# Layer 1 of a graph-attention kernel: the last five rows of the sorted tiles placed behind the last masks, with the closing of the last dense group between them

## The reference

```
# adj: 8192 x 8192, about 8 neighbours in each row, and the node itself
h = relu(layernorm(x));  Wh = h @ W
x = x + leaky_relu(softmax(where(adj, e_left + e_right.T, -1e9)) @ Wh, 0.2)       # layer 0
h = relu(layernorm(x))
e = leaky_relu(h @ a[:d] + (h @ a[d:]).T, 0.01)
x = x + softmax(where(adj, e, -9e15)) @ h                                         # layer 1
```

## Time and profile before

| | before |
|---|---|
| median of 3 runs (lowest, highest) | 1690.48 us (1688.31, 1691.74) |
| the profiled execution | 1689.47 us |
| its span, first to last instruction | 1687.3 us |
| busy: PE, DVE, ACT, POOL | 1551.5, 1255.9, 989.5, 562.5 us |
| first gather of layer 1 starts, last one starts | 1070.41, 1668.87 us |

### The profile page before, as it was taken

How to read it: one execution, slowest core, us unless ns; L and a number is a source line. 1 busy time by engine, 2 the same in 40 slices (tenths; PEclk the granted TensorE clock), 3 DMA queues, 4 the chain that set the end, 5 groups by cost and what they waited for, 6 DMA issues and landing times. The chain is left out here.

```text
span 1687.3 us, 37172 instructions
## 1 busy us (share of the span) xinstructions
PE 1551.5 (92%) x13443; PEld 1321.8 (78%) x13443; DVE 1255.9 (74%) x4759; ACT 989.5 (59%) x1514; POOL 562.5 (33%) x588
## 2 busy tenths in 40 slices
PE   6877999999999999999999999486898999989897
PEld 5645888888888888888888888365687877878786
DVE  6577998998898899887874453696866666666765
ACT  5978656665765566566666661675645445444542
POOL 0000000000000000000014554587777777777776
PEclk9998999999999999999999999798899999999999
DMA  9418989888988898898889994555444444444443
GB/s 318 172 43 341 348 303 364 320 301 313 369 310 300 329 358 310 301 374 319 331 337 385 393 361 112 178 132 153 119 135 114 130 123 129 115 142 117 128 113 107
DMA packets 141700, 406.91 MB, mean 241 GB/s; under 512 B 25857, under 2 KB 91586, under 8 KB 108834
## 3 DMA queue, kind: packets, MB, share of 16 engines
q1 hardware_dynamic: 116114, 335.11, 54.0%
q0 software_dynamic: 25488, 70.77, 14.7%
HBM read 365.39 MB, written 40.41 MB: 241 GB/s over the span
## 5 line engine op out<-in xcount | busy, mean ns | idle before, releaser
L1016 PE MATMUL banks<-HV,adjT 128*128 128x257 f16 x8192 | 938.8, 274 | 18.0 <-DVE adjT L673 10.2
L1016 PEld LDWEIGHTS banks<-HV,adjT 128*128 128x128 fp8e4 x8192 | 791.2, 97 | 150.8 <-DVE HV L703 23.8
L1746 PE MATMUL banks<-Vp,adjp 128*128 128x257 f16 x2304 | 451.9, 278 | 77.5 <-DVE adjp L1561 62.5
L458 ACT ACTIVATE adj_f<-adj_i 128x2048 fp8e4<-128x2048 int32 x256 | 480.1, 1898 | 5.6 <-DMA adj_i<-in_adj 5.5
L1334 POOL DMA_INDIRECT gat<-h_of_layer,rec x393 | 420.5, 1070 | 121.9 <-issue 115.3
L1746 PE MATMUL banks<-Vn,adjn 128*128 128x257 f16 x2304 | 451.0, 278 | 0.0
L1746 PEld LDWEIGHTS banks<-Vp,adjp 128*128 128x128 fp8e4 x2304 | 225.0, 99 | 121.7 <-issue 56.2
L440 POOL DMA_DIRECT2D xr<-x_after_layer x46 | 25.6, 557 | 834.4 <-DVE rank L941 772.5
L1746 PEld LDWEIGHTS banks<-Vn,adjn 128*128 128x128 fp8e4 x2304 | 227.1, 99 | 36.6
L1369 ACT ACTIVATE adjn<-h1bc,nh 128x384 fp8e5<-128x384 f32 x384 | 202.4, 604 | 0.0
L1390 ACT ACTIVATE e<-gat,hb 128x4 f32<-128x4 f32 (+3 forms) x168 | 41.2, 293 | 240.7 <-DMA gat<-h_of_layer,rec 240.5
(11 more groups left out here) (172 smaller groups left out, 1472.6 us busy)
## 6 DMA issues: line engine op xcount, KB each, us to landing
adj_i<-in_adj SPq DMA_DIRECT2D x256, 1024.0 KB, 7.2
h_of_layer<-hh SPq DMA_DIRECT2D x64, 129.0 KB, 6.6
hs<-h_of_layer SPq DMA_DIRECT2D x64, 129.0 KB
xt<-in_x SPq DMA_DIRECT2D x64, 128.0 KB, 7.0
packed_adj<-pk SPq DMA_DIRECT2D x64, 128.0 KB, 6.2
x_after_layer<-x SPq DMA_DIRECT2D x64, 128.0 KB, 7.0
HV<-in_x SPq DMA_DIRECT2D x14, 512.0 KB, 8.8
gat<-h_of_layer,rec POOLq DMA_INDIRECT x393
```

The source lines that it names most:

```text
L458: nc.scalar.activation(adj_f[:, b, q * QC:(q + 1) * QC], adj_i[:, q, :], ACT.Copy, scale=2.0, saturate=False).then_inc(conv_done, 1)
L1016: last = nc.tensor.matmul(acc[b][:, 0:DV], adjT_h[:, b, i, q, :, h], V0[:, jb, s, 0:DV], start=(jb == 0 and s == 0), stop=(jb == T - 1 and ...
L1746: mm = nc.tensor.matmul(bank[2 * i + part][:, 0:DV], m[:, i * P:(i + 1) * P], V[:, j, s, 0:DV], start=(j == 0 and s == 0), stop=(j == T - ...
```

## The change

The table `rows_by` is made with a longer total: `REST` = 1.25 chunk units are added to its divisor. `rows_by[96]` is then 388 in place of 393, and every earlier entry is the old one or up to five rows lower (the first that differs is `rows_by[13]`, 57 for 58). Five rows stand behind the 96 chunks: two of them, then `take_sums` of the last group, one row, `add_negatives`, and the last two with the finishing of the last tiles. ACT's list gets the two calls of `weigh` that go with it.

```
--- before.py
+++ after.py
@@ -1074,6 +1074,7 @@
         LEAD = 3
         FIRST = 1.25
         HEAD = 0.25
+        REST = 1.25
         OUT_LAG = 5
         NOUT = 6
         NACC = 3
@@ -1090,8 +1091,10 @@
         last = [max(k for k in range(len(batch)) if batch[k][0] == m) for m in range(NS)]
         fills = [sum(batch[i][2] - batch[i][1] for i in range(k % NBUF, k + 1, NBUF)) for k in range(len(batch))]
         pace = [max(0.0, FIRST * min(n, NC) + max(0, n - NC) - HEAD) for n in range(C)]
-        rows_by = [len(row) * a / pace[-1] for a in pace]
+        rows_by = [len(row) * a / (pace[-1] + REST) for a in pace]
         rows_by = [0] + [int(a + 1e-6) for a in rows_by]
+
+        assert len(row) - rows_by[C] > 3
 
         def lead_of(q):
 
@@ -1442,7 +1445,9 @@
                         weigh(k0, lead_of(q1))
                     if n + 2 < NC:
                         halves(n + 2)
+                weigh(lead_of(rows_by[C]), lead_of(rows_by[C] + 2))
                 scale_sums(NGD - 1, NGD == 1)
+                weigh(lead_of(rows_by[C] + 2), len(batch))
                 with act.If(act.value_load(redi[0:1, 0:1]) > 0):
 
                     def dense(g, g2, n_in, tail):
@@ -1699,8 +1704,11 @@
                         add_rows(min(q0 + 2, q1), q1)
                     else:
                         add_rows(q0, q1)
+                add_rows(rows_by[C], rows_by[C] + 2)
                 take_sums(NGD - 1)
+                add_rows(rows_by[C] + 2, rows_by[C] + 3)
                 add_negatives(NGD - 1)
+                add_rows(rows_by[C] + 3, len(row))
                 with dve.If(dve.value_load(redi[0:1, 0:1]) > 0):
 
                     def dense(g, tail):
```

## The result

The changed kernel takes 1696.13 us in the median of 10 executions (1691.28 to 1703.63), the kernel before 1690.13 in 10 on the same chip: 6.0 us between the medians. The ratio on record, taken over all these executions, is 1.0038, interval 1.0025 to 1.0051, so 6.4 us longer (4.2 to 8.6); such ratios are used from here on. The profiled execution took 1695.83, with a span of 1693.6 and a granted clock of 0.969. The sign and the road were forecast; 3.13 us of the size were, and about as much again was not.

What follows compares the result with a forecast made beforehand. POOL's gapless list of gathers and scatters was taken to bound the kernel. Fewer rows 0, earlier last masks 0 and the moved closing 3.13 us gave 1693.6 us on the median of 1690.48; range 1690.6 to 1696.6, widened for rivals to 1688.5 to 1698.5.

Steps and rivals of the forecast that it cites:

- The sorted road: End of kernel: tile 45's finishing, its scatter, then POOL's closing; claimed to end the span, 8.05 us behind the last scatter.
- The dense road: End of kernel: DVE's closing, then SP's stores; as rival it ends the kernel, time 1690.7 us, chance 0.18.
- POOL's 22%: POOL's share of the whole span on the chain of waits, claimed to be nearly all of layer 1's part.
- The closing, 3.13 us: DVE's `take_sums` and `add_negatives` of the last group, moved ahead of the last rows; claimed to delay the last scatter 3.13 us.
- The last masks a batch earlier, 0: Last chunks' masks on DVE: PE ends sooner, but DVE still waits for the last batch; gain 0.
- Fewer rows per chunk, no waiting: POOL's gathers in layer 1: rows up to five later, 2.3 us of slack left, so no wait, cost 0.
- The unknown is how masks fall on gathers: Stretch of POOL's gathers from 1205 to 1670 us, 20.7 us before; change taken as 0, with 3 us for the range.
- nothing in the order favours one side: Argument against the rival that masks fall on gathers less often (1686.7 us, chance 0.07): mask number is the same.

Runs made afterwards that it cites:

- e3: The change itself, run again and timed against the kernel before: 1694.74 us, +7.1 us (4.6 to 9.6).
- e2: Kernel before with its table up to the last chunk, but the closing placed between the last rows as in the change: 1693.32 us, +6.6 us (4.4 to 8.8).
- e11: Kernel before with its table's last five entries lowered by one to five rows, closing last: 1688.21 us against 1688.99, −0.8 us (−2.9 to 1.4).
- e12: The change's pace and end, closing last, masks in 71 of 75 chunks as far behind the weights as before: 1690.04 us, +0.8 us (−1.7 to 3.2).
- e10: The change's table through entry 93, the table of before for the last three entries, closing last: 1691.72 us, +4.1 us (1.9 to 6.3) against before.
- e1: The change's table, but all rows ahead of the closing as before: 1693.24 us against 1687.44 for the kernel before, +5.1 us (2.9 to 7.3).
- e9: Kernel before, entries 19 to 93 moved by at most one row to places where masks had stretched gathers most: +5.7 us (3.7 to 7.8).
- e8: Kernel before, entries 19 to 93 moved by at most one row to places where masks had stretched gathers least: 1690.47 us, +1.2 us (−0.7 to 2.9).
- e6: The change without the scatters of tiles 43, 44 and 45 and SP's wait for them; ran once, span ending at 1687.8 us.

## Why the prediction was right in its sign and short in its size

- **The sorted road ends the kernel.** Right: 8.04 us from the last scatter's end to the span's end in every profile that has the last scatters, and 7.8 us won when they are left out. The dense road ended well ahead. Two readings on the way were loose. POOL's 22% is three fifths of layer 1's part of the span (about 37%), four fifths with the pauses put down to issue, and not nearly all. And POOL's DRAIN ends at 1687.07 in the time of the rows, 7.81 us behind the last scatter and not 7.87; neither moves the sum.
- **The closing, 3.13 us.** Right: 3.13 in the first profile and in e3. Its place was right too; it didn't wait for PE, which e2 shows would have cost 1.34.
- **The last masks a batch earlier, 0.** Right as far as can be told: e11, −0.8 (−2.9 to 1.4).
- **Fewer rows per chunk, no waiting.** Right: the one long pause for rows was 1.3 us in the change and 2.2 in e3, 2.6 before, and e12, with fewer rows, measured +0.8 (−1.7 to 3.2).
- **"The unknown is how masks fall on gathers … I take 0 for it."** This is the step that failed, in size: it measured +4.1 us (1.9 to 6.3) in e10 and +5.1 in e1. With it the sum is 3.1 + 4.1 − 0.8 = 6.4, where 3.1 was forecast; 1696.13 lies at the upper edge of the forecast's own range, 1690.6 to 1696.6. The range held because its 3 us were worked out from just this unknown. It was taken as a draw anew at each piece, with 0 for its mean. What the runs show is no chance of the execution: a table has its own stretch, which repeats in part from one execution to the next (chunk 88), so e9's table, by one row off that of before, costs 5.7 us. DVE takes a batch's weights when its gathers and exponentials are there, and the rows between the weights and the masks move the masks against the gathers of the next batches. The order of before and after could have told that the meeting would change (28 chunks one row behind the weights for 13), but neither the sign nor the price, as e8's miss shows; that "nothing in the order favours one side" was not refuted by any count, only by measuring.
- What stays open: which instant of a gather must be free of the mask instructions, for the unpacking and the row additions too, and so a rule that prices a table ahead of a run. Also why fewer rows with most of the old places (e12) have as many held gathers as the change and yet came out near before. And the 1.54 us by which the last gather's data came late in the profile of the change and in e1's (5.22 us) and not in e3's.

## What to carry to other kernels

Where one engine's list is the bound and another's instructions lengthen its instructions, moving the second engine's work "in its shadow" is not free even when nothing waits: here a move by one row at most was worth 5.7 us (e9). See at which step behind their common wake-up the moved instructions stand, before and after; where that changes, the cost can change by an amount that these counts did not give, so measure a table with the places moved and the pace kept. And before work is moved ahead of the last rows, follow both roads to the end of the span: here 8 us of closing stand behind the one road's last transfer, and 4.4 us behind the other's last instruction.

## What the runs showed of the hardware that was not expected

POOL's closing has a length of its own: 8.04 us from the last scatter's end to the end of the record in 13 profiles whatever else was late, and 7.57 from there to the DRAIN's end in e6. The Trainium skill, "VectorE: DVE Perf Modes", section "The DRAIN you can't avoid", has about 12 ns for the DRAINs of the pre- and postamble on all engines. The other engines' last ones are recorded with 70 to 90 ns in e6, POOL's with 9.2 us in the profile of the change, 7.81 of them behind its last scatter's end. It stands at a line of the kernel, like the one of 7.58 us at the end of layer 0, so it may not be of the kind that the page means.

And the lock between an exclusive or on DVE and a gather on POOL has two sharp sides, 0.33 us behind its start and 0.22 us behind its end, so that its price turns on tenths of a microsecond.
